# A routed feed-forward kernel: sorted rows packed without a gap, a half tile at the seam, and new orders on all engines

## What is computed

```python
x = x + tanh(g_xattn) * xattn(layernorm(x), ctx)      # 16 heads of 16, 77 keys of width 192 a batch
x = x + tanh(g_ffn)   * ffn(layernorm(x))
# ffn: 2 experts and a shared pair of layers, 256 -> 1024 -> 256
top1   = argmax(softmax(xf @ gate_w.T))
masked = xf[None] * one_hot(top1).T[:, :, None]
h      = relu(einsum('end,edh->enh', masked, w1) + b1[:, None, :])
out    = (einsum('enh,ehd->end', h, w2) + b2[:, None, :]).sum(axis=0) + relu(xf @ sw1 + sb1) @ sw2 + sb2
```

## Time and profile before

| | us |
|---|---|
| runs (3) | 352.51 median, 351.61 to 352.97 |
| profiled execution | 354.73, its span 353.0 |
| PE busy | 323.2 (92% of the span) |
| DVE / ACT / POOL busy | 223.5 / 217.3 / 197.1 |
| mean granted PE clock | 0.971 |
| sorted part (235.0 to 342.4) | 107.4 |

### The profile page before, as it was taken

How to read it: one execution, slowest core, us unless ns; L and a number is a source line. 1 busy time by engine, 2 the same in 40 slices (tenths; PEclk the granted TensorE clock), 3 DMA queues, 4 the chain that set the end, 5 groups by cost and what they waited for, 6 DMA issues and landing times.

```text
span 353.0 us, 7375 instructions
## 1 busy us (share of the span) xinstructions
PE 323.2 (92%) x2407; PEld 288.8 (82%) x2407; DVE 223.5 (63%) x490; ACT 217.3 (62%) x491; POOL 197.1 (56%) x274
## 2 busy tenths in 40 slices
PE   7984769889999999999999989999999999999970
PEld 6662658667989778797889969999999999999970
DVE  6999578999889657668957925334354435343540
ACT  3565586976785866847948553546655656464640
POOL 7467578673765478537480785244553544464432
PEclk9999588999999999999999999999999999999996
DMA  6999695280515241203330210212311321022110
GB/s 193 293 308 240 107 315 146 71 212 4 143 34 120 43 92 58 72 3 120 121 119 2 68 53 30 88 34 63 89 60 30 89 78 37 25 71 88 49 41 30
DMA packets 40230, 33.88 MB, mean 96 GB/s; under 512 B 16697, under 2 KB 37709, under 8 KB 40205
## 3 DMA queue, kind: packets, MB, share of 16 engines
q1 hardware_dynamic: 36552, 25.80, 27.2%
q0 software_dynamic: 2816, 7.09, 6.3%
q10 hardware_dynamic: 837, 0.67, 0.7%
HBM read 21.72 MB, written 12.35 MB: 97 GB/s over the span
## 4 chain that ended last, share of the span: by engine, by line
PE 67%; DVE 10%; DMA 6%; POOL 5%; SPq 4%; issue 3%; ACT 1%; another core or an unknown queue 1%; ACTq 0%; POOLq 0%; DVEq 0%
PE y_ps L1405 23%; PE h_ps L1405 16%; PE s_ps L1405 11%; PE bank L1405 10%; DMA x_all<-in_x 5%; PE bank L1538 4%; SPq L516 1%; DVE smax L1173 1%; POOL sorted_dram L667 1%; PE bank L1642 1%; DVE rsum L1191 1%; SPq L458 1%; DMA k_own<-k_dram 1%; POOL hT_lo L676 1%; POOL nt L692 1%
## 5 line engine op out<-in xcount | busy, mean ns | idle before, releaser
L1371 DVE TENSOR_TENSOR hT_lo<-h,hT_hi 128x256 fp32r<-128x256 f32 x72 | 32.5, 452 | 45.2 <-ACT h L1027 42.1
L648 POOL TENSOR_TENSOR probs<-probs,rinv 128x616 f32<-128x616 f32 x32 | 41.4, 1293 | 27.6 <-DVE rinv L1195 27.5
L1024 ACT ACTIVATE hT_hi<-h_ps,vec_cols 128x256 fp32r<-128x256 f32 x36 | 17.1, 475 | 43.3 <-PE h_ps L1405 39.9
L1405 PE MATMUL y_ps<-ew_hi,hT_hi 128*128 128x256 f32 x144 | 41.5, 288 | 0.0
L1405 PE MATMUL y_ps<-ew_hi,hT_lo 128*128 128x256 f32 x144 | 40.3, 280 | 0.0
L1405 PE MATMUL y_ps<-ew_lo,hT_hi 128*128 128x256 f32 x144 | 40.3, 280 | 0.0
L937 ACT ACTIVATE hT_hi<-h_ps,vec_cols 128x512 fp32r<-128x512 f32 (+1 forms) x40 | 24.7, 617 | 24.8 <-PE h_ps L1405 24.4
L1405 PE MATMUL y_ps<-sw_hi,hT_hi 128*128 128x256 f32 x128 | 38.1, 297 | 1.8 <-POOL hT_lo L676 1.7
L777 POOL DMA_INDIRECT out<-final,scatter_token x18 | 19.6, 1092 | 29.9 <-issue 16.2
L1405 PE MATMUL y_ps<-sw_lo,hT_hi 128*128 128x256 f32 x128 | 36.1, 282 | 0.0
L1405 PE MATMUL y_ps<-sw_hi,hT_lo 128*128 128x256 f32 x128 | 36.1, 282 | 0.0
(11 more groups left out here) (197 smaller groups left out, 1054.8 us busy)
## 6 DMA issues: line engine op xcount, KB each, us to landing
v_diag<-v_rows SPq DMA_DIRECT2D x16, 256.0 KB
stage<-in_L_ffn_w SPq DMA_DIRECT2D x4, 1024.0 KB, 5.4
sorted_dram<-empty_rows SPq DMA_DIRECT2D x10, 257.0 KB, 8.9
xs<-sorted_dram SPq DMA_DIRECT2D x10, 257.0 KB
stage<-in_L_ffn_sw SPq DMA_DIRECT2D x2, 1024.0 KB, 7.1
x_all<-in_x SPq DMA_DIRECT2D x1, 1536.0 KB, 10.3
part_dram<-x_all SPq DMA_DIRECT2D x3, 512.0 KB
k_dram<-probs SPq DMA_DIRECT2D x2, 616.0 KB, 10.2
```

The lines of the kernel that those rows point to most:

```text
L648: nc.gpsimd.tensor_tensor(pq, pq, rinv[:, b % 2, k, :].unsqueeze(2).to_broadcast([P, HG, KEYS]), ALU.mult).then_inc(p_ready, 1)
L1024: nc.scalar.activation(hT[0][:, c % HB, 0:RTOK], hidden_bank(c % 4)[:, 0:RTOK], ACT.Relu, bias=b1_sb[:, 1 + e, c:c + 1]).then_inc(h_hi, 1)
L1371: nc.vector.tensor_tensor(hT[1][:, c % HB, 0:RTOK], h32[:, c % 2, 0:RTOK], hT[0][:, c % HB, 0:RTOK], ALU.subtract).then_inc(h_lo, 1)
L1405: return nc.tensor.matmul(out_, lhsT, rhs, start=start, stop=stop, **kw)
```

## The change

Slots are now exactly 2048. Row tiles are eight. Where the seam lies in the second half of a tile, the tile is run with expert 0, where it lies in the first half, with expert 1; the 128 rows of that half are run once more with the other expert, as a half tile behind the loops. Its weights are copied, by a register that holds the expert, over those of the shared layers. It scatters only its own expert's rows, after all other rows are out. A ninth round is run only where the seam lies in the first or in the last 128 rows. Only the 256 rows behind the slots are filled. Names are `plan` (five numbers: rounds with expert 0, rounds, whether tile 0 runs twice, the half, its expert) and `half_...`. All five orders are new, `LO_ON_POOL` has three chunks for five, `FOLDED` ten quarters for eleven; the scaling of the bias rows is a step (`bc`) of its own on POOL; the wait for the fills goes from POOL's first scatter to SP, in front of its loop.

```diff
-RTILES = TOKENS // RTOK + 1
-SLOTS = RTILES * RTOK
+RTILES = TOKENS // RTOK
+MOST_ROUNDS = RTILES + 1
...
-LO_ON_POOL = (1, 3, 4, 5, 6)
-FOLDED = {2, 4, 11, 12, 16, 19, 22, 23, 26, 28, 31}
+LO_ON_POOL = (1, 4, 5)
+FOLDED = {2, 4, 11, 12, 16, 19, 25, 29, 30, 31}
...
-    ct.3.1 h.3.0 h.3.1 oth.0 h.3.2 y.3.0 h.3.3 h.3.4 y.3.1 h.3.5 y.3.2 y.3.3 ct.4.1 h.3.6 h.3.7 n2.4.0.0 y.3.4
-    y.3.5 h.4.0 h.4.1 y.3.6 y.3.7 h.4.2 h.4.3 xst.1 y.4.0 h.4.4 y.4.1 y.4.2 h.4.5 h.4.6 y.4.3 h.4.7 y.4.4 y.4.5
-    y.4.6 y.4.7
+    h.3.0 h.3.1 ou.7.0 y.3.0 h.3.2 h.3.3 y.3.1 h.3.4 h.3.5 y.3.2 y.3.3 ct.3.1 h.3.6 y.3.4 h.3.7 n2.4.0.0 y.3.5
+    ct.4.1 y.3.6 y.3.7 h.4.0 oth.0 h.4.1 h.4.2 y.4.0 h.4.3 h.4.4 y.4.1 y.4.2 h.4.5 y.4.3 h.4.6 xst.1 h.4.7 y.4.4
+    y.4.5 y.4.6 y.4.7
...
-    di.7.3 hl.19 hl.20 ro.3.0 ro.3.1 hl.21 ro.3.2 ro.3.3 hl.22 ro.4.0 ro.4.1 scat.3 hl.25 ro.4.2 ro.4.3 hl.27
-    hl.28 hl.29 scat.4 hl.30 hl.33 hl.35 hl.36 hl.37 hl.38
+    ro.3.1 ro.3.2 ro.3.3 hl.25 ro.4.0 ro.4.1 hl.28 ro.4.2 hl.29 ro.4.3 scat.3 scat.4 hl.33 hl.36 hl.37
...
-    fl.0 fl.1 kw.0 vz.0 vz.1 kw.1 fl.2 fl.3 kr.1 kr.2 vw.0 fl.4 vw.1 wd.0 wd.1 vr.0 kr.3 vw.2 vr.1 wd.3 kr.4
-    vr.2 vw.3 wd.2 vw.4 kr.5 vr.3 vr.4 vw.5 kr.6 vr.5 vw.6 ps.0 vw.7 kr.7 vr.6 vr.7 ps.1 wd.4 wd.5 ps.2 xs ps.3
-    ps.4
+    fl.0 kw.0 vz.0 vz.1 kw.1 kr.1 kr.2 wd.0 vw.0 wd.1 vw.1 vr.0 kr.3 vw.2 vr.1 vr.2 kr.4 vw.3 wd.3 vw.4 vr.3
+    kr.5 vr.4 wd.2 vw.5 vw.6 vr.5 kr.6 vw.7 ps.0 kr.7 vr.6 vr.7 ps.1 wd.4 wd.5 ps.2 ps.3 xs ps.4
 """
...
             sp.wait_ge(seam_rdy, 1)
-            tiles_of_0 = sp.value_load(tiles0_int[0:1, 0:1], min_val=1, max_val=RTILES - 1)
-
-            def routed(j):
+            sp.wait_ge(filled, 16)
+            rounds = sp.value_load(plan_int[0:1, ROUNDS:ROUNDS + 1], min_val=RTILES, max_val=MOST_ROUNDS)
+            again = sp.value_load(plan_int[0:1, AGAIN:AGAIN + 1], min_val=0, max_val=1)
+            shared_half = sp.value_load(plan_int[0:1, SHARED_HALF:SHARED_HALF + 1], min_val=0, max_val=TILES - 1)
+            half_expert = sp.value_load(plan_int[0:1, HALF_EXPERT:HALF_EXPERT + 1], min_val=0, max_val=1)
+
+            with sp.Fori(0, rounds - 1) as j:
                 sp.wait_ge(xsT_ps, j + 1)
                 sp.wait_ge(ids_copied, j + 1)
-                load_sorted(j + 1)
-
-            with sp.Fori(0, tiles_of_0) as j:
-                routed(j)
-            with sp.Fori(tiles_of_0, RTILES) as j:
-                routed(j)
-            sp.wait_ge(xs_in, 16 * (RTILES + 1))
+                load_sorted(j + 1 - again)
+            sp.wait_ge(xsT_ps, rounds)
+            sp.wait_ge(ids_copied, rounds)
+            sp.dma_start(xs[:, 0, :], sorted_dram[bass.ds(shared_half * P, P), :]).then_inc(xs_in, 16)
+            sp.dma_start(half_b1[:, :], b1_sb[:, bass.ds(1 + half_expert, 1), :].rearrange("p o c -> p (o c)")
+                         ).then_inc(half_in, 16)
+            sp.wait_ge(other_rdy, 1)
+            sp.dma_start(half_other[:, :], other_row[:, bass.ds(1 - half_expert, 1), :].rearrange("p o d -> p (o d)")
+                         ).then_inc(half_in, 16)
...
+            pool.wait_ge(half_ids, 1)
+            pool.indirect_dma_start(
+                out=half_part[:, :], out_offset=None, in_=part_dram[:, :],
+                in_offset=bass.IndirectOffsetOnAxis(ap=half_token[:, 0:1], axis=0),
+                bounds_check=last_token, oob_is_err=False).then_inc(half_gathered, 16)
+            pool.wait_ge(half_gathered, 16)
+            pool.wait_ge(half_in, 16 * 2)
+            nc.gpsimd.tensor_tensor(half_part[:, :], half_part[:, :], half_other[:, :], ALU.add).then_inc(half_added, 1)
+            pool.wait_ge(half_ids, 2)
+            pool.wait_ge(half_done, 1)
+            pool.indirect_dma_start(
+                out=out[:, :], out_offset=bass.IndirectOffsetOnAxis(ap=half_token[:, 1:2], axis=0),
+                in_=half_final[:, :], in_offset=None, bounds_check=last_token, oob_is_err=False).then_inc(half_out, 16)
+            pool.wait_ge(half_out, 16)
 
...
+            half_expert = act.value_load(plan_int[0:1, HALF_EXPERT:HALF_EXPERT + 1], min_val=0, max_val=1)
+
+
+            act.wait_ge(y_used, CHUNKS_SHARED)
+            for n in range(2, 6):
+                act.wait_ge(w_lo[n], 1)
+            for n in range(2):
+                act.dma_start(sw1_sb[n][:, :, :].rearrange("p k h -> p (k h)").bitcast(F32),
+                              ew[:, bass.ds(half_expert, 1), n, :].rearrange("p o h -> p (o h)").bitcast(F32)
+                              ).then_inc(half_w, 16)
+                act.dma_start(sw2_sb[n][:, :, :].rearrange("p k d -> p (k d)").bitcast(F32),
+                              ew[:, bass.ds(half_expert, 1), 2 + n, :].rearrange("p o h -> p (o h)").bitcast(F32)
+                              ).then_inc(half_w, 16)
 
...
+            act.wait_ge(half_in, 16 * 2)
+            for c in range(HC):
+                act.wait_ge(half_sum, c + 1)
+                if c < HB:
+                    act.wait_ge(y_used, rounds * HC + CHUNKS_SHARED)
+                else:
+                    act.wait_ge(half_y, c - HB + 1)
+                nc.scalar.activation(hT[0][:, c % HB, 0:P], h32[:, c % 2, 0:P],
+                                     ACT.Relu, bias=half_b1[:, c:c + 1])
+                if c >= 2:
+                    act.wait_ge(half_lo, c - 1)
+                nc.scalar.activation(h32[:, c % 2, P:2 * P], h32[:, c % 2, 0:P], ACT.Relu, bias=half_b1[:, c:c + 1]
+                                     ).then_inc(half_32, 1)
 
 
...
+            def half_hidden(c):
+
+                if c == 0:
+                    dve.wait_ge(h_lo, rounds * HC + LO_DVE)
+                dve.wait_ge(half_h, c + 1)
+                if c >= 2:
+                    dve.wait_ge(half_lo, c - 1)
+                nc.vector.tensor_reduce(out=h32[:, c % 2, 0:P],
+                                        in_=hidden_bank(c % 4)[:, 0:2 * P].rearrange("p (m s) -> p s m", m=2),
+                                        axis=AX_X, op=ALU.add).then_inc(half_sum, 1)
+
+            def half_hidden_lo(c):
+
+                dve.wait_ge(half_32, c + 1)
+                nc.vector.tensor_tensor(hT[1][:, c % HB, 0:P], h32[:, c % 2, P:2 * P], hT[0][:, c % HB, 0:P],
+                                        ALU.subtract).then_inc(half_lo, 1)
+
+            half_hidden(0)
+            dve.wait_ge(xs_in, rounds * 16 + 16)
+            nc.vector.tensor_copy(half_token[:, 0:1], xs[:, 0, DIM:ROW]).then_inc(half_ids, 1)
+            dve.wait_ge(seam_step, SEAM_OPS + 4)
+            nc.vector.tensor_tensor(half_token[:, 1:2], xs[:, 0, DIM:ROW], half_drop[:, :], ALU.add).then_inc(half_ids, 1)
+            for c in range(1, HC):
+                half_hidden(c)
+                half_hidden_lo(c - 1)
+            half_hidden_lo(HC - 1)
+            dve.wait_ge(half_y, HC)
+            dve.wait_ge(half_added, 1)
+            dve.wait_ge(rows_out, rounds * 32)
+            nc.vector.scalar_tensor_tensor(out=half_final[:, :], in0=y_ps[:, 0, :], scalar=gains[:, 1:2],
+                                           in1=half_part[:, :], op0=ALU.mult, op1=ALU.add).then_inc(half_done, 1)
...
+            pe.wait_ge(xsT_lo, rounds + 1)
+            pe.wait_ge(half_w, 16 * 4)
+            for n in range(HC + 3):
+                if n < HC:
+
+                    if n < 4:
+                        pe.wait_ge(h_32, rounds * HC + (CHUNKS_SHARED + n - 3))
+                    else:
+                        pe.wait_ge(half_sum, n - 3)
+                    for kc in range(KC):
+                        both = xsT_parts[:, :, bass.ds(rounds % 2, 1), kc, 0:P].rearrange("p m o s -> p m (o s)")
+                        for m in range(2):
+                            ins = mm(hidden_bank(n % 4)[:, 0:2 * P], sw1_sb[m][:, kc, n * P:(n + 1) * P], both,
+                                     kc == 0 and m == 0, kc == KC - 1 and m == 1)
+                    ins.then_inc(half_h, 1)
+                if n >= 3:
+                    c = n - 3
+                    pe.wait_ge(half_lo, c + 1)
+                    if c == 0:
+                        pe.wait_ge(final_rdy, rounds)
+                    ins = cut(y_ps[:, 0, :], lambda m: hT[m][:, c % HB, 0:P], lambda m: sw2_sb[m][:, c, :], c == 0,
+                              c == HC - 1, skip_group_check=True)
+                    ins.then_inc(half_y, 1)
...
```

More of the change, by code:

```diff
@@ L57 @@
 WARM = (10, 5)
-FILLS = 5
+FIRST, ROUNDS, AGAIN, SHARED_HALF, HALF_EXPERT = range(5)
+SEAM_OPS = 7
 UNITS = [[0], [1, 2], [3, 4], [5, 6], [7]]
@@ L508, in weights_in, with fill @@
                              source.rearrange("(k p) h -> p k h", p=P)).then_inc(w_in[n], 16)
-            def fill(n):
+            def fill():
                 sp.wait_ge(empty_made, 2)
-                share = (RTILES + 1) // FILLS
-                for j in range(n * share, (n + 1) * share):
-                    rows = sorted_dram[j * RTOK:(j + 1) * RTOK, :].rearrange("(t p) d -> p t d", p=P)
```

(5 more changed lines are left out.)

220 lines of the change are left out of this document (134 added, 86 removed).

## The result

The changed kernel takes 350.86 us (median of 18 runs, 348.32 to 355.42) against 352.14 for the kernel before (18 runs): a ratio of 0.9937, 95% interval 0.9916 to 0.9957. The forecast was 343.2 with a range that ended at 351.0. The direction is right; the size is not: 1.3 us of 9.3 by the medians, 2.2 by the ratio.

A forecast was written before the change was run, and what follows sets the result against it. TensorE was taken as the bound from 90 to 180 us and in the sorted loop, SyncE's DMA queue as late before 90. Terms -5.5 - 0.5 - 3.7 + 2.0 - 1.6 = -9.3 gave 343.2 us by the median; range 336.5 to 351.0.

The forecast's parts named there:

- a: Start, SyncE's queue: one fill of ten ends TensorE's wait for k_own; 5.5 us saved, between 0 and 9.2.
- b: Shared part: new engine orders and fewer hidden-row chunks on POOL; net 0.5 us saved, bounds -1.7 to +5.
- cap of 5.8 us: Start, 31 to 46 us: VectorE's idle time, 0.69 + 5.11 us, taken as the most it can close up.
- c: Sorted-row loop: the ninth round goes, saving 11.9 us with TensorE never idle.
- d: Behind the loop: the half tile adds 8.2 us, bounds 6.6 and 11.9.
- e: First sorted round: four 1 MB weight copies on ACT stall TensorE 2.0 us, bounds 0 and 13.8.
- slower rival: First sorted round: second xs load queues behind all 4.19 MB; cost 13.8 us in place of 2.0, total 355.0; chance 0.11.
- f: Kernel's end: one scatter in place of two and a final over 256 columns; together 1.6 us saved.
- The start gives all: Start: TensorE gets its whole 9.2 us back and the copies cost nothing; 337.5 us; chance 0.14.
- The sorted rows come late: Before the sorted loop: xs load, now behind ps.3, up to 5.1 us late; 3.6 gives 346.8; chance 0.13.

## Why the prediction was wrong

*a and b, the start.* "I take 5.5" for the fills and "-0.5" for the orders are wrong as a split. Their sum, -6.0, is too small against the profiles' -9.4, and not clearly wrong against the 5 to 8 us that the medians leave. The steps at the queue were right: issues at 22.57 (forecast 23.5 at the latest), no wait for k_own. Two signs failed: the clock was to stay at 1.00 from 31 to 46 and stood at 0.83 behind 36, and 90 to 180 was to be as full as before and lacked 1.2 us. What failed in the account is to price the two one by one. The cap of 5.8 us from VectorE's idle time in the earlier trace rows was a cap under the old VectorE list; the change brought another. Alone the fill is worth 2.4 at most, the orders 2.5 at most, and 5 or more come only with both.

*c, the ninth round, and d, the half tile.* -3.7 forecast, -3.68 measured. In parts: -11.84 for the round, +8.77 for the half (8.2 forecast), and -0.6 over seven rounds of 11.75 for 11.84. The half's first product waits 0.63 us for the subtraction, as the chain through ACT and VectorE was put.

*e, the copies.* This is the step that failed and that the miss comes from: 2.0 forecast, 10.95 measured, 9 us against a miss of 7.7. Four parts of it were too low. ACT was to issue in 4 x 0.37 = 1.5 us; it took 4.02, and TensorE lost 2.99 where "under 0.7" stood. The load beside full traffic was to land 5.2 us after its issue, the value of x_all's row, whose neighbours had for the most part packets of 1 KB as it did; it was turned 9.6 us after it, since its first packet moved only after 4.3 us (cause open) and then its packets of 1 KB went one for one with packets of 8 KB. The issue itself came 2.3 us late (at 233.08; 230.60 without copies), since SyncE's four register reads took 3.77 us beside the copies for 1.43. And the clock, which the forecast counted only in its slower rival, took 3.3 us after the two stalls. The range of this term, 0 to 13.8, did hold it.

*f, the end.* -1.6 forecast, -1.8 measured.

*The rivals.* The slower case named the place and nearly the size (13.8 for 10.95), and it stood at 0.11. That the kernel still came out faster is 2.9 us less lost here than in that rival, and a start that gave somewhat more than the 6.0 with which the rival was added up. So the direction was right by a margin of 1 to 2 us that the forecast's main cost, off by 9, could as well have used up: that part is luck. The slower case's mechanism, the load queued behind all 4.19 MB, is half right: it moves in turns, but late and slowly enough to land when they end. "The start gives all" has 9.2 for the start, near the profiles' 9.4, but from the fill alone, which gives about a quarter of it at most, and it had the copies cost nothing. "The sorted rows come late" did not happen here, and did with the old engine lists.

## What to carry to other kernels

A large copy placed where "nobody needs the queue" was paid here by the next small transfer on whichever queue, by register reads and by the clock, and in bytes the large packets won every turn. Cut it into pieces and put them into rounds that are full of compute; 0.5 MB a round cost nothing measurable here, and whether the first round had a piece made no difference in the ratio. Price an edit that removes a wait and one that reorders the engines together: here each alone gave a quarter or less of what both gave. And when a term's range is 0 to 14 us, its lower part is no forecast: look at what the priced row's neighbours were before taking it.
